# Macaron block: FFN passes over pairs of batches, another order of the opening, row maxima split before their transposition, two score banks and one PV bank

## The chip, the cores and the metric

One core of a Trainium2 chip runs the whole block. The metric is the device time in microseconds of one execution. Its engines each work through a queue of their own in order: TensorE (matmuls, with a sequencer that waits on semaphores), VectorE, ScalarE, GpSimd, and SyncE, which here only issues DMAs. They meet at semaphores alone.

## The reference

x is 8 batches of 512 tokens of 256 numbers, float32. Three steps follow each other, each behind a layer norm:

```python
x = x + 0.5 * ffn(layernorm(x))            # "first"
x = x + attn(layernorm(x))                 # rms norm, 16 heads of 16, causal softmax, Wo, + its own input
x = x + 0.5 * ffn(layernorm(x))            # "second", same weights
# ffn: 2 experts, FF = 1024; a token goes to the expert with the larger logit:
sel = argmax(softmax(x @ gate_w.T));  h = silu(x @ w_gate[sel].T) * (x @ w_up[sel].T)
out = (h @ w_down[sel].T) * probability of sel
```

## The kernel before, in words

**Order.** One function, `master()` (L113 and on), gives every piece of work a place on a scale of points and sorts by it; each engine then walks through the same sorted list and does its own part of each item. So the order is written by hand, and an engine that must wait holds all that is behind it on its queue. The loop is unrolled.

**FFN.** A pass takes one batch: its 512 tokens are sorted by expert, 640 places (5 slots of 128), expert 0 from the front and expert 1 from the back. A slot that may hold both experts' border takes its weights by a register (`flags`, `expert`). Each slot is two units (q = 0, 1) of half of FF; a unit is 48 gate and up matmuls of 128 columns (float32 as two float16 parts, three products), tanh on ScalarE (L628), two products on VectorE (L819, L823), a split into two parts on ScalarE (L634) and GpSimd (L579), and 12 down matmuls of 256 columns (L1028 to L1030). 16 passes (8 batches, first and second) of 10 units are 160 units, 6 points each. `PASSES` gives their order, `PASS_AT` their points.

**Route.** Ahead of a pass, `ROUTE_STEPS`: statistics on VectorE, their scale on GpSimd, normalisation on ScalarE (L608), dot products with the difference of the two gate rows on VectorE (L778), a prefix sum over tokens on TensorE (L981, L983, into ps_m), places (L797), four scatters on GpSimd (L538), one transposing load on SyncE (L444) into x_t. After the pass, four gathers on GpSimd (L553, `y_gather`) and the update of x on VectorE (L811, `x_update`).

**Attention.** Each batch is four parts (four heads each) of two pairs of heads; a pair is five fills of a PSUM bank. For each fill TensorE makes the scores (L1073, mask L1075) in ps_s, VectorE reduces them to row minima of the negated scores (L891, L895). At the part's end the minima are transposed on TensorE (L1081, `row_max`), split in three bf16 parts on VectorE (L904 to L908), saved to DRAM and loaded as three more rows of qt by three DMAs (L479, L482), so that the second, transposed scores (L1092, L1094, ps_st) come out with the maximum subtracted. ScalarE takes exp twice (L704, L705), VectorE or GpSimd the low part (L913, L584), TensorE multiplies with V (L1109, ps_v), VectorE normalises each pair (`o_norm`: L922, L924, L928). Part p starts at point 115 + 23 p. ps_s has one bank, ps_v two in turn; ps_m is shared by projections (L944), transposes, prefix sums and row maxima, each waiting until the one before is read.

**Opening.** The weights are loaded; VectorE finds the largest of the gate and up weights, then of the down weights, each gives a power of two as scale (`w_scale`, nine small instructions with a transpose L973 and a broadcast L975 on TensorE), and ScalarE and VectorE split 14 pieces into two parts (`w_split`, L599, L752). x_sorted is zeroed from x_t, which GpSimd sets to zero first; it also fills v_parts with ones.

## Time and profile before

| | us |
|---|---|
| median of 3 runs | 1386.37 (1385.54 to 1393.45) |
| profiled execution | 1373.07 |
| its span, first to last instruction | 1371.3 |
| TensorE, VectorE, ScalarE, GpSimd busy | 1139.5, 972.4, 710.8, 542.2 |
| mean granted TensorE clock | 0.938 of full |

The page shows one execution. Busy times are of instructions alone; a matmul's end is modelled, its time includes its way through the array, and the next one starts before it is over, so the distance from start to start tells the pace. The chain that ended last is cut short on this page at the last gather, so stages are read by windows.

### The profile page before, as it was taken

Reading aid. Unit: us, or ns where it says so; the run is one execution under the profiler, and the core shown is the slowest. Engines: PE = TensorE matmul, PEld = TensorE weight load, DVE = VectorE, ACT = ScalarE, POOL = GpSimd, SP = SyncE. Lnnn points to the kernel's source line nnn. Section 1 sums busy time; section 2 is a strip of 40 time slices with the busy share of each in tenths; the row PEclk is TensorE's granted clock in tenths of the full one; section 3 lists DMA queues with packets and bytes.
Section 4 is the critical chain, followed back from the end, with each engine's and each line's share of the span. In section 5 each row is a group of like instructions: output and inputs, shape, how many; then the busy total and the mean of one; then the engine's idle time right before and its main releaser. Section 6 shows DMA issues by size and latency. Waiting matters only on the chain. (4 is left out here: it accounts for less than half of the span.)

```text
span 1371.3 us, 40339 instructions
## 1 busy us (share of the span) xinstructions
PE 1139.5 (83%) x15028; PEld 983.4 (72%) x15028; DVE 972.4 (71%) x2064; ACT 710.8 (52%) x1311; POOL 542.2 (40%) x681
## 2 busy tenths in 40 slices
PE   0588889999888978899798888988999988989485
PEld 0467777777767866778587777876878877778374
DVE  7743548887786786888787878777888876766322
ACT  1523425656555654655465556645666654556221
POOL 6144344335425243344342434434445253344422
PEclk9999999999999999999899999999999999999788
DMA  9002222332123112322042223211312323120211
GB/s 324 6 25 63 84 80 65 79 100 74 49 64 92 39 39 78 106 71 65 28 119 60 68 73 89 78 35 54 108 41 72 98 62 70 33 58 32 44 39 43
DMA packets 118869, 96.21 MB, mean 70 GB/s; under 512 B 56096, under 2 KB 112672, under 8 KB 118688
## 3 DMA queue, kind: packets, MB, share of 16 engines
q1 hardware_dynamic: 101024, 66.36, 17.9%
q0 software_dynamic: 6144, 16.79, 4.2%
q10 hardware_dynamic: 11520, 10.49, 2.4%
q8 instruction: 134, 2.20, 0.7%
q14 instruction: 47, 0.39, 0.1%
HBM read 45.75 MB, written 37.36 MB: 61 GB/s over the span
## 5 line engine op out<-in xcount | busy, mean ns | idle before, releaser
L579 POOL TENSOR_TENSOR h_lo<-hid,h_hi 128x256 bf16<-128x256 f32 x320 | 223.1, 717 | 584.0 <-ACT h_hi L634 583.4
L704 ACT ACTIVATE area<-ps_st 128x512 f32<-128x512 f32 x320 | 189.8, 593 | 229.6 <-PE ps_st L1094 229.1
L1009 PE MATMUL ps_g<-x_t,w 128*128 128x128 f16 x1280 | 244.8, 226 | 31.2 <-DMA x_t<-x_sorted 14.5
L1011 PE MATMUL ps_u<-x_t,w 128*128 128x128 f16 x1280 | 245.7, 224 | 0.0
L1009 PE MATMUL ps_u<-x_t,w 128*128 128x128 f16 x1280 | 245.3, 224 | 0.2
L1011 PE MATMUL ps_g<-x_t,w 128*128 128x128 f16 x1280 | 245.1, 226 | 0.0
L1010 PE MATMUL ps_g<-x_t,w 128*128 128x128 f16 x1280 | 243.7, 225 | 0.0
L1010 PE MATMUL ps_u<-x_t,w 128*128 128x128 f16 x1280 | 243.4, 222 | 0.0
L895 DVE TENSOR_REDUCE row_min<-ps_s 128x1 f32<-128x512 f32 (+2 forms) x384 | 183.2, 504 | 60.7 <-PE ps_s L1075 60.1
L913 DVE TENSOR_TENSOR area<-area 128x512 f16<-128x512 f32 x256 | 186.8, 730 | 4.4 <-ACT area L705 2.1
L705 ACT ACTIVATE area<-ps_st 128x512 f16<-128x512 f32 x320 | 189.7, 593 | 0.0
L1028 PE MATMUL ps_y<-wd,h_hi 128*128 (+1 forms) x640 | 183.2, 286 | 6.9 <-POOL h_lo L579 6.4
L1029 PE MATMUL ps_y<-wd,h_hi 128*128 (+1 forms) x640 | 183.6, 287 | 0.0
L1030 PE MATMUL ps_y<-wd,h_lo 128*128 (+1 forms) x640 | 183.6, 287 | 0.0
L1009 PEld LDWEIGHTS ps_g<-x_t,w 128*128 (+1 forms) x1280 | 128.6, 101 | 51.5 <-issue 21.1
L1073 PE MATMUL ps_s<-kt,qt 96*128 96x512 bf16 (+3 forms) x512 | 138.9, 310 | 32.0 <-DVE row_min L895 31.0
L628 ACT ACTIVATE hid<-ps_g,g_scale 128x512 f32<-128x512 f32 x160 | 109.8, 686 | 103.8 <-PE ps_g L1011 100.4
L819 DVE SCALAR_TENSOR_TENSOR hid<-hid,ps_g 128x512 f32<-128x512 f32 x160 | 108.4, 677 | 68.8 <-ACT hid L628 68.8
L1092 PE MATMUL ps_st<-qt,kt 99*128 99x512 bf16 (+3 forms) x512 | 137.6, 307 | 10.6 <-ACT area L705 8.4
L1009 PEld LDWEIGHTS ps_u<-x_t,w 128*128 (+1 forms) x1280 | 126.6, 99 | 17.9 <-issue 2.4
L1011 PEld LDWEIGHTS ps_g<-x_t,w 128*128 (+1 forms) x1280 | 128.8, 101 | 2.3 <-issue 0.4
L1010 PEld LDWEIGHTS ps_g<-x_t,w 128*128 (+1 forms) x1280 | 129.1, 101 | 1.1
(146 smaller groups left out, 2636.5 us busy)
## 6 DMA issues: line engine op xcount, KB each, us to landing
qk_scratch<-area SPq DMA_DIRECT2D x32, 384.0 KB, 2.5
qt<-qk_scratch SPq DMA_DIRECT2D x192, 64.0 KB, 2.8
kt<-qk_scratch SPq DMA_DIRECT2D x192, 64.0 KB, 2.8
y_sorted<-ys ACTq DMA_DIRECT2D x80, 128.0 KB, 1.7
x_buf<-x SPq DMA_DIRECT2D x8, 512.0 KB, 4.9
out<-x_buf SPq DMA_DIRECT2D x8, 512.0 KB, 3.0
area<-w_down SPq DMA_DIRECT2D x4, 512.0 KB, 13.1
qt<-max_scratch SPq DMA_DIRECT2D x96, 4.0 KB
```

What stands on the lines that cost most here:

```text
L579: pool.tensor_tensor(h_lo[:, u % 2, c], hid[:, u % 2, c], h_hi[:, u % 2, c], ALU.subtract).then_inc(h_lo_done, 1)
L704: act.activation(p_f32[:, f % 3], ps_st[:], ACT.Exp, scale=-1.0)
L705: act.activation(p_hi[:, f % 4], ps_st[:], ACT.Exp, scale=-1.0).then_inc(exp_done, 1)
L895: ins = dve.tensor_reduce(row_min[:, p % 2, i, h + hh:h + hh + 1], ps_s[:, at:at + P * (i + 1)], AX.X, ALU.min)
L913: dve.tensor_tensor(p_lo[:, f % 4], p_f32[:, f % 3], p_hi[:, f % 4], ALU.subtract).then_inc(lo_done, 1)
L1009: pe.matmul(cols, w_hi, x_hi, start=kb == 0 and f == 0, stop=False, skip_group_check=True)
L1010: pe.matmul(cols, w_hi, x_lo, start=False, stop=False, skip_group_check=True)
L1011: ins = pe.matmul(cols, gate_up(u, kind, 1, kb, q * QF + f), x_hi, start=False, stop=kb == KB - 1, skip_group_check=True)
L1028: pe.matmul(ps_y[:, 0:D], hi, wd_lo, start=q == 0 and f == 0, stop=False, skip_group_check=True)
L1029: pe.matmul(ps_y[:, 0:D], hi, wd_hi, start=False, stop=False, skip_group_check=True)
L1030: ins = pe.matmul(ps_y[:, 0:D], lo, wd_hi, start=False, stop=q == 1 and f == QF - 1, skip_group_check=True)
L1073: pe.matmul(ps_s[:, at:at + keys], qt[0:ROWS, h, i * P:keys], kt[0:ROWS, h, 0:keys], start=n == 0, stop=False, skip_group_check=True)
```

## The change

Batches 2 and 3, 4 and 5 of the first FFN, first 7 with second 2, and second 3 with 4 are passed in pairs: 1024 tokens sorted together into 9 slots. 12 passes have 76 slots and 152 units. The route is done for each batch (an item), the second of a pair with the counts of the first added in the prefix sum; one transposing load follows. Route steps are spaced wider and start earlier, parts of attention stand 21 points apart instead of 23. In the opening, ScalarE sums the absolute down weights of each piece (`accum_out`) in place of VectorE's maximum, the second scale and most splits stand behind the first unit, zeroing takes a block of yt by 5, 9 and 4 DMAs, and only the ones column of v_parts is set. The row maxima are split by VectorE as 128 x 16 (`max_parts`), then all three parts are transposed by one bf16 matmul, copied by ScalarE, saved by one DMA and loaded by one. ps_s gets two banks in turn, ps_v keeps one. x gets a sixth buffer, routes a fourth.

```diff
-PASSES = [("first", 0), ("first", 1), ("first", 2), ("first", 3), ("first", 4), ("second", 0), ("second", 1),
-          ("first", 5), ("second", 2), ("first", 6), ("first", 7), ("second", 3), ("second", 4), ("second", 5),
-          ("second", 6), ("second", 7)]
-PASS_OF = {what: n for n, what in enumerate(PASSES)}
-XBUFS = 5
-ROUTES = 3
+
+PASSES = [[("first", 0)], [("first", 1)], [("first", 2), ("first", 3)], [("first", 4), ("first", 5)], [("second", 0)],
+          [("second", 1)], [("first", 6)], [("first", 7), ("second", 2)], [("second", 3), ("second", 4)],
+          [("second", 5)], [("second", 6)], [("second", 7)]]
+ITEMS = [(n, i, what, b) for n, batches in enumerate(PASSES) for i, (what, b) in enumerate(batches)]
+ITEM_OF = {(what, b): k for k, (n, i, what, b) in enumerate(ITEMS)}
+SLOTS = [T * len(batches) + 1 for batches in PASSES]
+
+ITEM_AT, SLOT_AT = [0], [0]
+for batches, slots in zip(PASSES, SLOTS):
+    ITEM_AT.append(ITEM_AT[-1] + len(batches))
+    SLOT_AT.append(SLOT_AT[-1] + slots)
+UNITS = [(n, s, q) for n, slots in enumerate(SLOTS) for s in range(slots) for q in range(2)]
+MAX_SLOTS = max(SLOTS)
+PLACES = MAX_SLOTS * P
+XBUFS = 6
+ROUTES = 4
...
-PASS_POINTS = UNIT_POINTS * UNITS
-PASS_AT = [PASS_POINTS * n for n in range(15)] + [916]
+SLOT_POINTS = 2 * UNIT_POINTS
+PASS_AT = [SLOT_POINTS * at for at in SLOT_AT[:4]] + [336, 396, 462, 522, 630, 738, 798, 865]
 PART_AT = 115
-PART_POINTS = 23
-FILL_POINTS = 2.3
-LEAD = 27
+PART_POINTS = 21
+FILL_POINTS = PART_POINTS / 10
+LEAD = 33
+PAIR_LAG = 9
...
+MAX_PARTS_AT = 21.5
...
-OUT_AT = [130.5, 132, 134, 136]
-ROUTE_STEPS = [("l_stats", 0, 0.0), ("l_stats", 1, 0.5), ("l_rstd", 0, 1.5), ("l_norm", 0, 3.0),
-               ("l_split", 0, 4.5), ("l_dlogit", 0, 4.6), ("l_exp", 0, 6.0), ("l_prefix", 0, 6.5),
-               ("l_pos", 0, 6.6), ("l_coef", 0, 7.8), ("l_scatter", 0, 9.0), ("l_load", 0, 13.0)]
+OUT_AT = [122, 123.5, 125.5, 127.5]
+ROUTE_STEPS = [("l_stats", 0, 0.0), ("l_stats", 1, 0.5), ("l_rstd", 0, 1.5), ("l_norm", 0, 4.0),
+               ("l_split", 0, 6.0), ("l_dlogit", 0, 6.5), ("l_exp", 0, 10.5), ("l_prefix", 0, 11.0),
+               ("l_pos", 0, 11.2), ("l_coef", 0, 13.0), ("l_scatter", 0, 14.5), ("l_load", 0, 19.0)]
...
-            ("l_pos", 0): -55.8, ("l_coef", 0): -43.2, ("l_scatter", 0): -55, ("l_load", 0): -54}
-SPLIT_AT = [-50, -49, -48, -47, -46, -45.5, -45, -44.5, -43, -42, -2, 0, 14, 16]
+            ("l_pos", 0): -55.8, ("l_coef", 0): 20, ("l_scatter", 0): -55, ("l_load", 0): -54}
+MAX_AT = [-59, -58, -57, -56, -55, -54, -53, -52, -51.2, -51, -46.8, -46.6]
+SCALE_AT = [-50.5, 3.9]
+SPLIT_AT = [-50, -49, -48, -47, -46, 1.2, 2.2, 4, 5, 7, 13, 15, 26, 28]
...
+    for k, (n, i, what, b) in enumerate(ITEMS):
+        end = PASS_AT[n] + SLOT_POINTS * SLOTS[n] + 5.2 * i
+        put(end + 8, "y_gather", k)
+        put(end + 13, "x_update", k)
+        at = PASS_AT[n] - LEAD - PAIR_LAG * (len(PASSES[n]) - 1 - i)
...
+        put(part_at(p, MAX_PARTS_AT), "max_parts", p)
         put(part_at(p, ROW_MAX_AT), "row_max", p)
...
-        ps_s, ps_st, ps_m = bank("ps_s"), bank("ps_st"), bank("ps_m")
-        ps_v = [bank(f"ps_v{n}") for n in range(2)]
-        ps_o = [v[:, 0:2 * T * VW].rearrange("p (h i c) -> p h i c", h=2, i=T) for v in ps_v]
+        ps_st, ps_v, ps_m = bank("ps_st"), bank("ps_v"), bank("ps_m")
+        ps_s = [bank(f"ps_s{n}") for n in range(2)]
+        ps_o = ps_v[:, 0:2 * T * VW].rearrange("p (h i c) -> p h i c", h=2, i=T)
...
-                    zero(0)
+                    sp.wait_ge(zero_ready, 1)
+                    zero(0, range(SLOTS[0]))
...
+                    sp.wait_ge(scattered, 64 * ITEM_AT[n + 1])
+                    if n >= 2:
+                        sp.wait_ge(u_done, 2 * SLOT_AT[n - 1])
+                    sp.dma_start_transpose(x_t_of(n), x_sorted[n % 2][0:P * SLOTS[n], :]).then_inc(xt_loaded, 16)
                     if n == 0:
-                        zero(1)
-                    sp.wait_ge(scattered, 64 * (n + 1))
-                    if n >= 2:
-                        sp.wait_ge(u_done, UNITS * (n - 1))
-                    sp.dma_start_transpose(x_t[n % 2][:], x_sorted[n % 2]).then_inc(xt_loaded, 16)
...
-                    sp.wait_ge(max_parts_done, p + 1)
-                    sp.dma_start(max_scratch[g].rearrange("r i h s -> (i h) r s"), max_parts[:]).then_inc(max_saved, 16)
+                    sp.wait_ge(max_rows_done, p + 1)
+                    sp.dma_start(max_scratch[g], max_rows[:]).then_inc(max_saved, 16)
                     sp.wait_ge(max_saved, 16 * (p + 1))
-                    for n in range(3):
-                        sp.dma_start(qt[ROWS + n:ROWS + n + 1, heads].rearrange("o h (i s) -> o h i s", i=T),
-                                     max_scratch[g, n:n + 1].rearrange("o i h s -> o h i s")
-                                     ).then_inc(max_in, 16)
+                    sp.dma_start(qt[ROWS:ROWS + 3, heads].rearrange("r h t -> r (h t)"),
+                                 max_scratch[g].rearrange("(r n) s -> r (n s)", r=3)).then_inc(max_in, 16)
...
-            pool.memset(x_t[0][:], 0.0).then_inc(zero_ready[0], 1)
+            pool.memset(yt[:, 0, :], 0.0).then_inc(zero_ready, 1)
...
-                        pool.memset(x_t[1][:], 0.0).then_inc(zero_ready[1], 1)
-                        link(pool.memset(v_parts[0][:], 1.0))
-                        pool.memset(v_parts[1][:], 1.0).then_inc(v_ones_ready, 1)
-                        pool.wait_ge(v_ones_ready, 1)
...
+                if what == "w_max" and st[1] >= GU_PIECES:
+
+                    w = st[1]
+                    act.wait_ge(w_in[w], 16)
+                    if w > GU_PIECES:
+                        act.wait_ge(w_sum_done, w - GU_PIECES)
+                    act.activation(flat(hid[:]), stage[w], ACT.Abs,
+                                   accum_out=w_max[:, w:w + 1]).then_inc(w_sum_done, 1)
...
+                elif what == "row_max":
+                    p = st[1]
+                    act.wait_ge(mt_done, p + 1)
+                    if p:
+                        act.wait_ge(max_saved, 16 * p)
+                    act.activation(max_rows[:], ps_m[0:3 * HG * T, 0:P], ACT.Copy).then_inc(max_rows_done, 1)
...
+                    ins = dve.tensor_tensor(place[r][:], high_place[:], ps_m[:, 0:T], ALU.add)
+                    if i == len(PASSES[p]) - 1:
+                        between = slice(0, SLOTS[p] - 2)
+                        ins = dve.scalar_tensor_tensor(out=of_slot[p % 3][:, between], in0=edges[:, between],
+                                                       scalar=ps_m[0:1, T:T + 1], in1=strides[:, between],
+                                                       op0=ALU.is_ge, op1=ALU.mult)
+                    ins.then_inc(l_pos, 1)
...
-                    if f == 0 and p >= 2:
-                        dve.wait_ge(mt_done, p - 1)
                     h = 2 * (f // KINDS)
                     if f % KINDS == KINDS - 1:
-                        ins = dve.tensor_reduce(row_min[:, p % 2, 1, h:h + 2], ps_s[:].rearrange("p (h n) -> p h n", h=2),
+                        ins = dve.tensor_reduce(row_min[:, p % 2, h:h + 2, 1], ps_s[f % 2][:].rearrange("p (h n) -> p h n", h=2),
                                                 AX.X, ALU.min)
                     else:
                         for hh, i, at in S_FILLS[f % KINDS]:
-                            ins = dve.tensor_reduce(row_min[:, p % 2, i, h + hh:h + hh + 1], ps_s[:, at:at + P * (i + 1)],
+                            ins = dve.tensor_reduce(row_min[:, p % 2, h + hh, i:i + 1], ps_s[f % 2][:, at:at + P * (i + 1)],
...
-                elif what == "row_max":
+                elif what == "max_parts":
                     p = st[1]
-                    dve.wait_ge(mt_done, p + 1)
+                    dve.wait_ge(max_done, FILLS * (p + 1))
                     if p:
-                        dve.wait_ge(max_saved, 16 * p)
-                    maxima = ps_m[0:T * HG, 0:P]
-                    link(dve.tensor_scalar(max_parts[:, 0, :], maxima, -1.0, None, ALU.mult))
-                    link(dve.scalar_tensor_tensor(out=max_rest[:], in0=maxima, scalar=-1.0, in1=max_parts[:, 0, :],
+                        dve.wait_ge(mt_done, p)
+                    minima = row_min[:, p % 2].rearrange("p h i -> p (h i)")
+                    link(dve.tensor_scalar(max_parts[:, 0, :], minima, -1.0, None, ALU.mult))
+                    link(dve.scalar_tensor_tensor(out=max_rest[:], in0=minima, scalar=-1.0, in1=max_parts[:, 0, :],
...
-                    if FILLS * p + f:
-                        pe.wait_ge(max_done, FILLS * p + f)
+                    if FILLS * p + f >= 2:
+                        pe.wait_ge(max_done, FILLS * p + f - 1)
...
-                    pe.wait_ge(max_done, FILLS * (p + 1))
-                    pe.transpose(ps_m[0:T * HG, 0:P], row_min[:, p % 2].rearrange("p i h -> p (i h)"), ident[:]).then_inc(mt_done, 1)
+                    pe.wait_ge(max_parts_done, p + 1)
+                    pe.matmul(ps_m[0:3 * HG * T, 0:P], max_parts[:].rearrange("p r n -> p (r n)"), ident16[:],
+                              start=True, stop=True).then_inc(mt_done, 1)
...
-                    if f % KINDS == 0 and n >= 2 * KINDS:
-                        pe.wait_ge(o_summed, n // KINDS - 1)
+                    if f % KINDS == 0 and n:
+                        pe.wait_ge(o_summed, n // KINDS)
```

## Rows read from the trace of the kernel before

**Rows 1.** Head of the page: busy time and share of the span by engine.

```profile
PE 1139.5 (83%) x15028; PEld 983.4 (72%) x15028; DVE 972.4 (71%) x2064; ACT 710.8 (52%) x1311; POOL 542.2 (40%) x681
```

**Rows 2.** Windows by stage: busy us (x instructions) of each engine, granted clock, DMA.

```profile
core 0: us, PE busy (x) PEld busy (x) DVE busy (x) ACT busy (x) POOL busy (x), PEclk, DMA share, GB/s
47.50:176.70 129.20, 106.66 (x1219) 92.92 (x1220) 59.53 (x124) 50.17 (x83) 46.81 (x67) 0.91 0.17 50
176.70:1268.60 1091.90, 967.23 (x13039) 833.76 (x13036) 844.66 (x1817) 625.46 (x1174) 442.20 (x540) 0.95 0.25 68
1000.00:1100.00 100.00, 92.17 (x1239) 79.67 (x1236) 85.14 (x185) 61.62 (x116) 40.12 (x51) 0.98 0.25 72
```

**Rows 3.** Waits of TensorE, 176.7 to 1268.6: us in total, times, longest.

```profile
PE ps_s L1073 <- DVE row_min L895: 31.0, 32, 4.6
PE ps_m L981 <- DVE neg_abs L788: 22.8, 6, 6.6
...
PE ps_m L944 <- DVE max_parts L908: 8.5, 6, 2.1
...
PE ps_m L981 <- DVE area L865: 8.2, 2, 5.4
```

**Rows 4.** The same, 47.5 to 176.7.

```profile
PE ps_m L981 <- DVE neg_abs L788: 10.8, 2, 5.5
```

**Rows 5.** Window of a stretch after a wait, columns as in rows 2.

```profile
403.00:409.80 6.80, 5.59 (x33) 4.14 (x33) 6.29 (x16) 1.91 (x4) 0.00 (x0) 0.50 0.42 122
```

**Rows 6.** Timeline, first gate matmuls of two units in succession: start, duration us.

```profile
1346.29 0.22 PE L1009 MATMUL ps_g<-x_t,w 128*128 128x128 f16 x1
...
1350.28 0.22 PE L1009 MATMUL ps_g<-x_t,w 128*128 128x128 f16 x1
```

**Rows 7.** Costliest groups by form, whole span: busy us, mean ns, idle before.

```profile
L823 DVE SCALAR_TENSOR_TENSOR hid<-hid,ps_u 128x512 f32<-128x512 f32 x160 | 109.9, 687 | 20.8 <-PE ps_u L1011 15.1 <-DVE hid L819 0.4
...
L819 DVE SCALAR_TENSOR_TENSOR hid<-hid,ps_g 128x512 f32<-128x512 f32 x160 | 108.4, 677 | 68.8 <-ACT hid L628 68.8
...
L640 ACT ACTIVATE ys<-ps_y 128x256 f32<-128x256 f32 x80 | 30.8, 385 | 76.2 <-PE ps_y L1030 76.0
...
L788 DVE SCALAR_TENSOR_TENSOR neg_abs<-dlogit 128x4 f32<-128x4 f32 x16 | 3.4, 213 | 0.0
```

**Rows 8.** Window of the mixed stage, VectorE's instructions on max_parts alone.

```profile
176.70:1268.60 1091.90, 41.18 (x128) 0.95 0.25 68
```

**Rows 9.** Timeline of the opening: start, duration in us.

```profile
25.72 3.50 DVE L733 TENSOR_SCALAR w_two<-w_exp 1x2 int32<-1x2 int32 x1
...
26.47 2.74 POOL L543 MEMSET v_parts<- 128x3136 bf16 x1
...
29.01 4.09 SPq L444 DMA_TRANSPOSE x_t<-x_sorted  x1
...
47.57 0.29 PE L1009 MATMUL ps_g<-x_t,w 128*128 128x128 f16 x1
...
54.70 0.10 PEld L1009 LDWEIGHTS ps_g<-x_t,w 128*128 128x128 f16 x1 [2.61 <-DVE hid L819]
```

**Rows 10.** DMA issues: count, median us to landing.

```profile
x_t<-x_sorted SPq DMA_TRANSPOSE x16, 6.4
```

**Rows 11.** Timeline of two handovers of PV: reciprocal and next PV.

```profile
845.20 0.36 PE L1109 MATMUL ps_v<-v_parts,area 128*128 128x49 bf16 x8
...
849.26 0.20 DVE L924 RECIPROCAL recip<-ps_v 128x8 f32<-128x8 f32 x1
...
1247.05 0.20 DVE L924 RECIPROCAL recip<-ps_v 128x8 f32<-128x8 f32 x1
...
1248.20 0.36 PE L1109 MATMUL ps_v<-v_parts,area 128*128 128x49 bf16 x8
```

**Rows 12.** TensorE's wait behind the last PV, and the last pass's first matmul.

```profile
PE ps_m L981 <- DVE neg_abs L788: 8.7, 1, 8.7
...
1305.91 0.29 PE L1009 MATMUL ps_g<-x_t,w 128*128 128x128 f16 x1 [13.05 <-DMA x_t<-x_sorted]
```

More of the change, by code:

```diff
@@ L217, in macaron @@
         xs = sb("xs", [P, T, 2, D], F16)
-        x_t = [sb(f"x_t{n}", [P, 2 * KB, PLACES], F16) for n in range(2)]
+        x_t = [sb(f"x_t{n}", [P, 2 * KB * PLACES], F16) for n in range(2)]
         ys = [sb(f"ys{n}", [P, D], F32) for n in range(2)]
@@ L715, in _ @@
                 what = st[0]
-                if what == "w_max":
+                if what == "w_max" and st[1] < GU_PIECES:
                     w = st[1]
@@ L998, in _ @@
                             pe.wait_ge(w_ready, GU_PIECES)
-                        if u % UNITS == 0 and what == "gate":
+                        if s == 0 and q == 0 and what == "gate":
                             pe.wait_ge(xt_loaded, 16 * (n + 1))
-                            pe.wait_ge(l_pos, n + 1)
+                            pe.wait_ge(l_pos, ITEM_AT[n + 1])
                         if u:
```

216 lines of the change are left out of this document (115 added, 101 removed).

## The prediction

> **What bounds the kernel now.** I read the head of the page, then the windows by stage, then TensorE's waits, then the costs on VectorE. The head [rows 1] says TensorE 83% busy, VectorE 71%: neither is full, so the bound must be looked for by stage. The windows [rows 2] cut the span at the first gate matmul (47.5 us), at the first score (176.7) and behind the last PV (1268.6). The stage from 176.7, attention interleaved with FFN, holds 1091.9 of 1371.3 us, with TensorE busy 967 and VectorE 845 us (77%). Its pace is not fixed: TensorE at 89% on the mean, in the stretch 1000:1100 both engines are higher, 92% and 85%. So the stage is limited by two in-order engines that wait for each other in turn, with slack to win when waits go.
>
> TensorE's waits in that stage [rows 3] are, of the 125 us that it stands idle there: 31.0 for the row-minimum reduction (S has one bank), 31.0 for the prefix matmul L981 (22.8 and 8.2), 8.5 for ps_m held by the row maxima; the rest is small. After such a stop the granted clock falls: the longest stop at the prefix in this stage that the projection's VectorE part ends, 5.4 us, is followed by 403.0 to 409.8 at 0.50, the lower level (1.2 GHz) [rows 3, 5]. The stage's mean is 0.95 [rows 2].
>
> **The change part by part.** The passes had 16 x 5 slots; now four pairs have 9 slots and eight single batches 5: 76 slots, 152 units for 160. One unit's TensorE work at the full clock is 48 gate and up and 12 down matmuls, from the first gate matmul at 1346.29 to the next unit's at 1350.28 [rows 6]: 4.0 us. On VectorE it is 677 + 687 ns [rows 7].
>
> Opening. Before, the first gate matmul (47.57) stands behind the second weight scale, because the order puts all of it first; the first scale itself is late by a VectorE instruction on two numbers that takes 3.50 us beside a memset on GpSimd and ends with it at 29.2 [rows 9]; the next one runs beside the next memset. These memsets go, the scan of the down weights goes to ScalarE, and the second scale and most splits go behind the first gate. Then what comes last is x_t: issued at 29.01, median 6.4 to landing [rows 9, 10], so 35.4. The splits are no later: the scale's chain started that instruction at 25.72 and is then some 1 us from its end, and the first splits need about 4 us behind it. Unit 0's gate and up matmuls hold two thirds of a unit's columns, 2.7 of the 4.0 us, and twice that at the lower clock, 5.4; its VectorE work ends near 41.5, the second scale, nine small instructions of some 0.21 us [rows 7], near 43.4, and unit 1 starts there against 54.70 [rows 9]: 11 us earlier. Several splits now stand between units on VectorE, which works 59.5 of 129 us in this stage [rows 2]; I take off 1. **Minus 10.** Its ends: minus 4 (if the work only moved behind unit 0 and is paid there; the memsets' part stays won) and minus 12 (35.4 against 47.6). Zeroing is now by 5, 9 and 4 DMAs from one small block, behind the load of pass 0: nothing waits for it until the scatter of pass 1; cover, the 60 us of pass 0.
>
> Route. Steps before the prefix matmul are spread over 11 points for 6.5, at a lead of 33 for 27. A point of the mixed stage is 1091.9/775 = 1.41 us (points 115 to 890), so the chain has 6 us more, and the longest wait is 6.6 [rows 3]. In the stage from 47.5 to 176.7 two waits cost 10.8 [rows 4]; I take three quarters, **minus 8**, as the extra item of the first pair is prepared there. In the mixed stage 31.0: I take two thirds, 20, plus 8 for the clock behind them. The bounds: nothing (the wait moves to the next user), and 31 + 3.4 x 8 = 58 when all go with their dips.
>
> For the clock the row says 0.95 over 1091.9 us, so 10% of the time was at the lower level. The Trainium skill's TensorE page (TensorE: Matmul & The Clock Gate, Terms) prices throttled time at its length times the share of pulses taken away. By that the stage would give back 55 us if no stop were left, not my 8; I hold to 8, as only a third of the stops are touched.
>
> Pairs. The mixed stage runs from point 115 to about 823 (parts every 21 points) instead of 890; with 6 points per unit it holds 118 units for 129. Eleven fewer at 4.0 us and 10% for clock and gaps: **minus 48**. The parts' own work stays. Ends: minus 0 (attention's chain has a pace of its own) and minus 15.0/0.77 = 19 if only VectorE's 11 x 1.364 counts, up to 67 x 1.41 = 94 (the pace per point kept, though each point holds more attention). I stay near the unit's TensorE time, as TensorE is the busier of the two. A transposing load of nine slots for five: 6.4 x 1.8 = 11.5 us [rows 10], issued 14 points = 20 us ahead: hidden. The sync queue is held by its issue for 4.09 x 1.8 = 7.4 us at most [rows 9]; the maxima behind it have 8 points = 11 us before the transposed scores: at no cost, and 2 us per hit if that cover goes (four pairs). Prefix matmuls of a second item: four more small ones, under 0.1 us each. The gather of a pair waits for nine slots, its deadline is 30 points away. A sixth x buffer only loosens.
>
> Row maxima. The four VectorE instructions of 16 x 128 take 41.2 us in 32 parts, 1.29 each part [rows 8]; they become four of 128 x 16, and the nearest row is one of 128 x 4 at 213 ns [rows 7]: 0.85 us at that price, at most the old 1.29. I take 0.7, since some of the like are shorter (the chain of nine above): 19 us less, off VectorE. A copy on ScalarE, at most 385 ns, the price of 128 x 256 [rows 7], x 32 = 12 us on an engine with 466 us idle in the stage [rows 2]. ps_m is held by the copy alone, so the 8.5 us of L944 go in part: **minus 3**. One load replaces three. The new copy waits for TensorE at the head of ScalarE's queue; behind it stand exp and tanh, which wait for TensorE anyway.
>
> Two S banks. A score fill waits for the reduction two fills back, 2.1 points = 3 us more slack, against waits of 31.0 in 32 pieces, longest 4.6 [rows 3]. Most go as waits at this place, but VectorE has the same work and is late at the next: I take 12; ends 0 and 31. The Trainium skill (same page, HAM oscillation — how this bites in real kernels) tells of a kernel where PSUM double buffering on top brought no further gain. By that the gain would be 12 us smaller; it is a rival below. The rows have a wait on this very bank, so I keep 12.
>
> One PV bank. The first PV of a pair must now wait for the reciprocal of the pair before. Before, it did not. Two handovers [rows 11]: in one the reciprocal ends at 1247.25 and the next pair's PV starts at 1248.20, 0.95 us of slack; in the other it ends at 849.46 and that PV started at 845.20, 4.3 us too early. So the price per handover lies between 0 and 4.3, 63 times. What stands behind the waiting PV is all of TensorE's queue: gates, scores, transposed scores, and so ScalarE's exp. I take 0.8 gross, nearer the calm one, 50 us, of which half is time in which TensorE would have waited for VectorE elsewhere: **plus 25**.
>
> Mixed stage: -48 - 20 - 8 - 3 - 12 + 25 = -66, 1026 us. VectorE's work there falls to 845 - 15 - 19 = 811, a share of 79%, between the two shown.
>
> Tail. From the last PV (1268.6) the chain of out-projection, statistics, prefix, load and gate (1305.91) lasts 37.3 us, with TensorE idle 8.7 and 13.05 us [rows 12]. Now pass 10 still has 5.8 units instead of 2: four more, 16 us, fit in those 21.7. The last pass and its way out stay. **Minus 3** for a shorter stop ahead of the last gate (0 to 6).
>
> Sum: -10 - 8 - 66 - 3 = -87. The profiled execution lasts 1373.07 us (span 1371.3), 13 under the runs' median of 1386.37; the same step from the median gives **1299**.
>
> **The rivals.**
> VectorE sets the pace: the mixed stage keeps its VectorE share of 77.4%: 811/0.774 = 1048, minus 44. Total -65: 1321. For it: VectorE is late in the handover at 849 [rows 11]; against: 85% in 1000:1100. Chance 0.20.
> The second S bank gives nothing, as VectorE is as late at the next place: -75, 1311. For it: the same reductions stay on a VectorE that is 77% busy; against: the waits on this bank are many and short [rows 3]. Chance 0.10. The page's sentence on PSUM buffers in the Trainium skill is of this kind.
> The waits really go, and the clock stays up: 85.1% everywhere, 953 us, -139, total -160: 1226. Against it: PV's bank. Chance 0.07. The skill's price of throttled time fits in this case alone.
> The change's fewer units buy nothing: attention's chain keeps 34.1 us per part and units only filled holes. Then -21 of opening, start and tail stay: 1365. For it: TensorE has 125 us idle in the stage; against: it is busy 89%. Chance 0.08.
> Slower: the single PV bank. Without it the sum is -112. Slower by 1% begins at 126/63 = 2.0 us net per handover; at 2.5 it is +158 - 112 = +46: 1432. It decides where VectorE's order has a route's or a projection's work ahead of the normalisation; the bank then stops TensorE, ScalarE's exp behind it comes late, and VectorE is late again. For it: the handover at 849; against: the other has slack. Chance 0.08.
>
> **How the numbers follow.** Forecast 0.47 with its own range 1270 to 1328 (opening 8, pairs 20, PV 25 either way, not all together). The range 1258 to 1352 leaves out the slower case, the 1365 one in part and most of the 1226 one. A difference under 1% can't be told from none here. Faster by more: 0.47 + 0.10 + 0.20 + 0.07 and a quarter of 0.08, 0.86 (the 1365 is 1.5% below, but its range reaches across 1%); within 1%: 0.06; slower: 0.08, the last rival's.
>
> **What would show it.** First gate near 35 to 38 and the first score near 157 to 160; 152 units on VectorE, 118 of them in the mixed stage; that stage near 1026; L981's waits under 15 us in all and the L1073 group's under 20; a new wait of the first PV on the reciprocal of 20 to 60 us; the maxima at under 0.25 us each. A mixed stage over 1060, or PV waits over 100 us, would prove the sum wrong.

## The result, and the profile after

The changed kernel's median is 1367.8 us (1365.91 to 1371.26, 4 runs) against 1387.49 of the kernel before (4 runs): a ratio of 0.9854 [0.9817, 0.989], 1.5% faster. 1299 was forecast, with a range from 1258 to 1352. The gain is a quarter of the forecast, and the time lies outside the range.

The windows by stage of the changed kernel, cut at its first gate matmul, first score and last PV (columns as in rows 2):

```profile
0.00:34.40 34.40, 0.86 (x8) 0.43 (x9) 22.32 (x46) 14.41 (x20) 12.26 (x39) 1.00 0.90 313
34.40:176.40 142.00, 113.04 (x1230) 96.77 (x1230) 71.56 (x158) 56.32 (x92) 56.65 (x76) 0.90 0.21 64
176.40:1261.70 1085.30, 926.36 (x12349) 795.75 (x12346) 821.09 (x1767) 613.72 (x1171) 418.56 (x508) 0.94 0.24 66
1261.70:1369.40 107.70, 82.19 (x987) 71.14 (x983) 35.58 (x70) 27.97 (x49) 36.42 (x49) 0.91 0.15 43
```

Against [rows 2]: the first gate comes 13 us earlier, the first score 0.3 us; the mixed stage is 6.6 us shorter, the tail 5.0 us longer. That is 1.9 us in all where the medians say 19.7, because the first trace of before was 13 us under its own runs and this one is 3.5 us over. So I profiled both again, on chips where before's median is 1370.5 and 1368.5; those two traces lie 3.9 and 5.2 us under the medians of their kernels, and the stages are compared in them. Before, second trace (mixed stage, tail):

```profile
176.80:1262.50 1085.70, 961.53 (x13039) 829.24 (x13037) 845.50 (x1817) 625.87 (x1174) 441.96 (x540) 0.96 0.25 68
1262.50:1364.80 102.30, 64.37 (x771) 56.18 (x767) 30.34 (x62) 22.20 (x39) 32.62 (x43) 0.82 0.17 42
```

Changed, second trace:

```profile
173.40:1232.90 1059.50, 907.73 (x12350) 782.86 (x12348) 824.76 (x1767) 613.93 (x1171) 419.08 (x508) 0.95 0.25 68
1232.90:1339.70 106.80, 82.82 (x986) 71.38 (x983) 35.80 (x70) 27.95 (x49) 36.42 (x49) 0.91 0.15 44
```

Of the 25.1 us between the spans (1364.8 and 1339.7), 3.4 lie ahead of the first score, 26.2 in the mixed stage, and the tail loses 4.5. In the mixed stage TensorE's busy time falls by 53.8 us, but its **idle time** (length less busy) rises from 124.2 to 151.8. That pair of numbers is what the rest of this document follows; in the first pair of traces it is 124.7 and 158.9. Busy time is no exact measure either: the same 12,350 matmuls of the mixed stage count as 904.6 to 926.4 us in nine traces with pairs, the 13,039 without pairs as 959.2 to 972.0 in six. So the fall in busy time is 41 us by the first pair of traces and 54 by the second, and a difference in idle time of less than some 15 us says little by itself. The units went as planned, and the waits did not.

TensorE's waits in the mixed stage of the changed kernel, first trace (columns as in rows 3):

```profile
PE ps_v L1163 <- DVE recip L972: 59.6, 31, 5.9
PE ps_st L1146 <- ACT area L748: 20.8, 15, 5.4
...
PE ps_v L1163 <- POOL area L612: 10.0, 5, 3.5
PE ps_m L1134 <- DVE area L915: 7.6, 7, 2.3
PE ps_m L992 <- DVE xt_lo L898: 6.1, 7, 1.5
...
PE ps_m L1031 <- DVE area L915: 3.2, 1, 3.2
...
PE ps_s L1126 <- DVE row_min L939: 2.5, 2, 1.8
```

Against [rows 3] the three waits that the change was to take away are nearly gone: S from 31.0 to 3.8 us (with a row of 1.3 for L943), the prefix (L1031 now) from 31.0 to 3.6, the row maxima (8.5) replaced by L1134's. In their place stands one wait of 59.6 us (61.5 in the second trace), of the first PV of a pair on the reciprocal. A handover is the way of the PV bank from its last reader, the reciprocal of one pair, to the first PV of the next. Counted over the 63 handovers, 39 first PVs start within 0.25 us of the reciprocal's end, so they had waited; before, 47 started ahead of it. The longest, on TensorE:

```profile
944.99 0.49 PE L1163 MATMUL ps_v<-v_parts,area 128*128 128x49 bf16 x8 [5.87 <-DVE recip L972]
```

and VectorE in the same stretch:

```profile
941.10 1.41 DVE L822 CUSTOM_DVE_ANT_0 junk<-xn_f,w_diff 128x256 bf16<-128x256 f32 x1
...
944.10 0.15 DVE L833 SCALAR_TENSOR_TENSOR neg_abs<-dlogit 128x4 f32<-128x4 f32 x1
944.18 0.55 DVE L970 TENSOR_REDUCE o_sum<-ps_v 128x128 f32<-128x384 f32 x1
944.64 0.20 DVE L972 RECIPROCAL recip<-ps_v 128x8 f32<-128x8 f32 x1
```

The route's dot products (3 us) stand ahead of the normalisation on VectorE, and TensorE stands for them. Then the clock falls; the windows behind it:

```profile
945.00:948.00 3.00, 3.00 (x28) 2.43 (x29) 1.43 (x4) 1.60 (x3) 0.17 (x1) 0.54 0.03 5
948.00:952.00 4.00, 4.00 (x79) 3.71 (x77) 2.47 (x5) 1.75 (x4) 2.29 (x3) 1.00 0.00 0
```

The opening of the changed kernel, VectorE (start, duration):

```profile
25.22 0.16 DVE L777 TENSOR_SCALAR w_two<-w_exp 1x2 int32<-1x2 int32 x1
...
42.01 0.69 DVE L873 SCALAR_TENSOR_TENSOR hid<-hid,ps_u 128x512 f32<-128x512 f32 x1
42.62 0.15 DVE L770 TENSOR_REDUCE w_max<-w_max 128x1 f32<-128x4 f32 x1
...
45.31 1.28 DVE L796 SCALAR_TENSOR_TENSOR w<-kt,w_scale,w 128x1024 f16<-128x1024 f32 x1
```

and TensorE:

```profile
34.39 0.27 PE L1062 MATMUL ps_g<-x_t,w 128*128 128x128 f16 x1 [8.58 <-issue]
...
46.80 0.28 PE L1062 MATMUL ps_g<-x_t,w 128*128 128x128 f16 x1 [1.97 <-issue]
```

The instruction on two numbers that took 3.50 us beside the memset [rows 9] takes 0.16 without it. Unit 0 starts at 34.4, unit 1 at 46.8 against 54.70.

### The profile page after: what moved, and what is told of

The parts are those of the page before. It is cut to its first block and busy times, and to the rows that moved or that the text cites. A ratio compares the mean times of both kernels' runs of the same rounds, so it can differ in the third digit from the quotient of the medians.

```text
span 1369.4 us, 39636 instructions
## 1 busy us (share of the span) xinstructions
PE 1122.4 (82%) x14564; PEld 964.1 (70%) x14564; DVE 950.5 (69%) x2040; ACT 712.4 (52%) x1331; POOL 523.9 (38%) x671
## 5 line engine op out<-in xcount | busy, mean ns | idle before, releaser
L607 POOL TENSOR_TENSOR h_lo<-hid,h_hi 128x256 bf16<-128x256 f32 x304 | 219.1, 741 | 582.1 <-ACT h_hi L671 580.6
L1062 PE MATMUL ps_g<-x_t,w 128*128 128x128 f16 x1216 | 240.4, 230 | 35.9 <-issue 27.3
L943 DVE TENSOR_REDUCE row_min<-ps_s 128x1 f32<-128x512 f32 (+2 forms) x384 | 183.3, 505 | 87.5 <-PE ps_s L1128 84.3
L1064 PE MATMUL ps_g<-x_t,w 128*128 128x128 f16 x1216 | 240.0, 230 | 3.1 <-issue 3.1
L1064 PE MATMUL ps_u<-x_t,w 128*128 128x128 f16 x1216 | 238.8, 226 | 2.9 <-issue 2.9
L1063 PE MATMUL ps_g<-x_t,w 128*128 128x128 f16 x1216 | 239.0, 229 | 1.9 <-issue 1.9
L1062 PE MATMUL ps_u<-x_t,w 128*128 128x128 f16 x1216 | 238.8, 227 | 2.1 <-issue 1.7
L1063 PE MATMUL ps_u<-x_t,w 128*128 128x128 f16 x1216 | 237.0, 225 | 1.2 <-issue 1.2
L961 DVE TENSOR_TENSOR area<-area 128x512 f16<-128x512 f32 x256 | 192.1, 750 | 11.7 <-ACT area L748 11.6
L1163 PE MATMUL ps_v<-v_parts,area 128*128 128x49 bf16 x2560 | 120.8, 187 | 76.1 <-DVE recip L972 59.6
L1081 PE MATMUL ps_y<-wd,h_hi 128*128 (+1 forms) x608 | 171.3, 282 | 6.2 <-POOL h_lo L607 3.9
L1163 PEld LDWEIGHTS ps_v<-v_parts,area 128*128 128x128 f16 x2560 | 102.8, 98 | 101.7 <-issue 50.8
L1083 PE MATMUL ps_y<-wd,h_lo 128*128 (+1 forms) x608 | 171.6, 282 | 0.0
L1082 PE MATMUL ps_y<-wd,h_hi 128*128 (+1 forms) x608 | 171.4, 282 | 0.0
L1062 PEld LDWEIGHTS ps_g<-x_t,w 128*128 (+1 forms) x1216 | 125.1, 103 | 55.9 <-issue 42.9
L1146 PE MATMUL ps_st<-qt,kt 99*128 99x512 bf16 (+3 forms) x512 | 140.3, 312 | 21.3 <-ACT area L748 20.8
L665 ACT ACTIVATE hid<-ps_g,g_scale 128x512 f32<-128x512 f32 x152 | 104.6, 688 | 92.8 <-PE ps_g L1064 72.7
L869 DVE SCALAR_TENSOR_TENSOR hid<-hid,ps_g 128x512 f32<-128x512 f32 x152 | 103.1, 678 | 62.3 <-ACT hid L665 62.3
```

Source lines behind the costliest of these rows:

```text
L607: pool.tensor_tensor(h_lo[:, u % 2, c], hid[:, u % 2, c], h_hi[:, u % 2, c], ALU.subtract).then_inc(h_lo_done, 1)
L943: ins = dve.tensor_reduce(row_min[:, p % 2, h + hh, i:i + 1], ps_s[f % 2][:, at:at + P * (i + 1)], AX.X, ALU.min)
L961: dve.tensor_tensor(p_lo[:, f % 4], p_f32[:, f % 3], p_hi[:, f % 4], ALU.subtract).then_inc(lo_done, 1)
L1062: pe.matmul(cols, w_hi, x_hi, start=kb == 0 and f == 0, stop=False, skip_group_check=True)
L1063: pe.matmul(cols, w_hi, x_lo, start=False, stop=False, skip_group_check=True)
L1064: ins = pe.matmul(cols, gate_up(u, kind, 1, kb, q * QF + f), x_hi, start=False, stop=kb == KB - 1, skip_group_check=True)
```

## The experiments

Two theories stood against each other after the result. **H**: the single PV bank, handed over late by VectorE, eats the gain. **V**: VectorE's pace is the bound, and each bank only shows where it is late. Ratios are to the kernel before, run beside them on the same chip; before's own median was 1389.7, 1370.5, 1368.5 and 1386.6 us on the four chips, so times of different chips are compared by ratio alone; figures in square brackets are 95% intervals. "Mixed" is the stage between first score and last PV, "idle" its length less TensorE's busy time.

**Banks as before, rest changed** (run twice).

```diff
-        ps_st, ps_v, ps_m = bank("ps_st"), bank("ps_v"), bank("ps_m")
-        ps_s = [bank(f"ps_s{n}") for n in range(2)]
+        ps_s, ps_st, ps_m = bank("ps_s"), bank("ps_st"), bank("ps_m")
+        ps_v = [bank(f"ps_v{n}") for n in range(2)]
...
-                    if FILLS * p + f >= 2:
-                        pe.wait_ge(max_done, FILLS * p + f - 1)
+                    if FILLS * p + f:
+                        pe.wait_ge(max_done, FILLS * p + f)
...
-                    if f % KINDS == 0 and n:
-                        pe.wait_ge(o_summed, n // KINDS)
+                    if f % KINDS == 0 and n >= 2 * KINDS:
+                        pe.wait_ge(o_summed, n // KINDS - 1)
```

> The changed kernel with the banks as before: S one, PV two in turn; all else as changed. Theory H (the handover of the one PV bank eats the gain): in the changed kernel TensorE waited 59.6 us for the reciprocal ahead of PV, before it did not, and the old waits on the S bank (31 us) come back; so 20 to 35 us faster than the changed kernel, 1333 to 1348, with the mixed stage near 1050. Rival P (the mixed stage has a pace of its own, about 34 us per part, and waits only move): within 8 us of the changed kernel, 1360 to 1376, with other waits of the same sum.

> The changed kernel with the banks as before, again, beside its base. Theory H: 10 to 20 us under the changed kernel, as between the first two calls (ratios 0.975 and 0.985). Rival: the two ratios came from different calls, and side by side they are within 5 us.

Measured: 1352.68, ratio 0.975 [0.9721, 0.978]; again, beside the changed kernel (0.9845 [0.9823, 0.9867]), 1340.46, 0.9809 [0.9764, 0.9854]. So the swap of banks costs 0.4 to 1.0% here, the lower figure (6.2 us, on one chip) with overlapping intervals. Its waits in the mixed stage (second run):

```profile
PE ps_s L1126 <- DVE row_min L943: 52.2, 40, 5.7
...
PE ps_s L1126 <- DVE row_min L939: 12.9, 6, 5.7
```

That is 65 us of waits on the one S bank (55.9 in the first run), where the changed kernel has 61.5 on the one PV bank. I read both as ways to wait for the same VectorE. Idle is 145.4 us here and 151.7 in the first run, against 151.8. Before, with the sparser order, that S bank cost 31.0 [rows 3].

**The swap alone, on the kernel before**, and **without pairs**: the old 16 passes, distances, lead and route steps, with new opening and row maxima, once with the new banks and once with the old.

```diff
-PASSES = [[("first", 0)], [("first", 1)], [("first", 2), ("first", 3)], ...
+PASSES = [[item] for item in [("first", 0), ("first", 1), ("first", 2), ...
-PART_POINTS = 21
+PART_POINTS = 23
-LEAD = 33
+LEAD = 27
```

> The kernel before with only the banks swapped: S two in turn, PV one. Theory H: handovers cost 60 to 80 us of TensorE stops against 31 saved, so 15 to 40 us slower than before, 1402 to 1427. Rival P: within 8 us of before, 1379 to 1395.

> The changed kernel without pairs: 16 passes of 5 slots, 160 units, with the points, the part distance of 23, the lead and the route steps of before; the opening, the row maxima and the banks are as changed. Theory H: the opening and the maxima give 10 to 15, the banks take 15 to 40: 1385 to 1415. Rival P: 1370 to 1387, as the opening alone shows.

> As the run without pairs, and with the banks as before too: before with the new opening and row maxima alone. Theory H: 1365 to 1378 (opening 13 us at the first gate, maxima 19 us less on VectorE). Rival P, with the opening's gain taken back ahead of the first score as in the changed kernel: 1380 to 1390.

Measured: the swap on the kernel before 1423.09, 1.0232 [1.0187, 1.0277]; without pairs 1394.01, 1.0024 [0.9996, 1.0052] with the new banks and 1376.34, 0.9911 [0.988, 0.9942] with the old. So the swap costs 2.3% on the kernel before, 1.1% without pairs and 0.4 to 1.0% in the changed kernel: it is a gain nowhere, and the same edit has three prices. On the kernel before the first PVs wait 61.3 us for the reciprocal and the 31.0 on S are gone, 30 more in all, and the time is 33 us longer. Opening and row maxima are worth 0.9%, 13 us. Mixed stage without pairs, new banks:

```profile
171.60:1281.90 1110.30, 959.19 (x13039) 825.79 (x13037) 840.05 (x1817) 630.77 (x1206) 443.48 (x540) 0.96 0.24 67
```

old banks:

```profile
173.40:1271.80 1098.40, 972.04 (x13040) 831.49 (x13038) 838.17 (x1817) 630.30 (x1206) 442.67 (x540) 0.96 0.24 67
```

Idle 151.1 and 126.4: near the value of before with the old banks, near the changed kernel's with the new. The one S bank waits 21.3 us in the second of them; its main row:

```profile
PE ps_s L1126 <- DVE row_min L943: 20.6, 27, 3.0
```

**Both kernels profiled again** (before, changed).

> The kernel before once more, for a second trace. Its first profiled execution was 13 to 16 us under the median of its timed runs, the other kernels' were within 10. If that execution was an exception, the second trace has a span near 1385 and a mixed stage near 1105 us; if it is how the traced execution always stands, near 1371 and 1092.

> The changed kernel itself once more. Two calls had medians of 1389.7 and 1370.5 us for the same kernel before, so only runs of one call are compared; this is the base for the three beside it. Both theories: 0.982 to 0.989 of before.

Measured: 1366.59 in one run, 3.9 us under the median of before on that chip, so the 13 us of the first trace were the exception; and 1346.70, 0.9845 [0.9823, 0.9867], close to the result's own ratio.

**Less work on VectorE by moving it** (banks as before; GpSimd makes two of five low parts instead of one), **less by leaving it out**, and **less work on TensorE**.

```diff
-                elif what == "p_lo" and st[2] % KINDS < KINDS - 1:
+                elif what == "p_lo" and st[2] % KINDS < KINDS - 2:
```

```diff
-                    dve.tensor_tensor(p_lo[:, f % 4], p_f32[:, f % 3], p_hi[:, f % 4],
+                    dve.tensor_tensor(p_lo[:, f % 4, 0:P], p_f32[:, f % 3, 0:P], p_hi[:, f % 4, 0:P],
```

```diff
-                        ins = pe.matmul(cols, gate_up(u, kind, 1, kb, q * QF + f), x_hi, start=False,
-                                        stop=kb == KB - 1, skip_group_check=True)
```

> The changed kernel with the banks as before, and with the low part of exp for two of five fills on GpSimd instead of one: 64 x 0.73 = 47 us less on VectorE, 64 x 1.19 = 76 more on GpSimd (38% busy). Theory V (the mixed stage follows VectorE's work: what it is late with, TensorE waits for at the next bank): 15 to 35 us faster than with the banks as before, 1318 to 1338. Rival H' (the stage follows the waiting hand-overs and latencies, not the amount of work): within 8 us of 1353, or slower, as the low part then comes 0.46 us later to PV.

> The changed kernel with VectorE making only the first 128 of the 512 columns of the low part of exp in its fills, the rest is zero: the output is less exact. VectorE has about 256 x 0.45 = 115 us less work. Theory V: 50 to 90 us faster. If TensorE's work sets the pace: under 20 us.

> The changed kernel without one of the three products (low weights by high x) of gate and up: its output is less exact. TensorE has 152 x 16 x 0.0557 = 135 us less to stream, nothing else changes. If TensorE's work sets the pace, 100 us or more faster: below 1268. Theory V: its work is half hidden, 40 to 75 us faster. If it is only the other engines, under 20.

Measured: 1348.91, 0.9881 [0.9815, 0.9947]; 1308.96, 0.9574 [0.951, 0.9637]; 1292.09, 0.9451 [0.9372, 0.9529]. Moving bought nothing over the banks as before (0.975 and 0.9809). It is a weak test of V, though: VectorE's busy time in the mixed stage is 801.3 us against 824.2 and 828.4 with the banks as before, 23 to 27 less for the 47 expected, because other instructions take longer (L822 726 ns for 625, a low part on VectorE 794 for 772). GpSimd needs 1.21 us for the low part:

```profile
L612 POOL TENSOR_TENSOR area<-area 128x512 f16<-128x512 f32 x128 | 154.3, 1210 | 74.4 <-ACT area L748 74.1
```

Mixed stage of the kernel with less VectorE work:

```profile
174.30:1200.80 1026.50, 904.60 (x12349) 781.83 (x12347) 719.77 (x1767) 613.41 (x1171) 397.35 (x508) 0.95 0.26 70
```

and with less TensorE work:

```profile
168.50:1202.50 1034.00, 832.50 (x10478) 701.33 (x10476) 829.27 (x1767) 611.22 (x1172) 418.66 (x508) 0.91 0.25 69
```

VectorE does 105 us less there than in the changed kernel and the ratio falls from 0.9845 by 0.027, 37 us of 1370 (28 to 46 by the intervals; V had 50 to 90): 0.35 us per us taken. TensorE loses 2,432 matmuls of 128 columns, 134 us at the 55 ns from start to start, and the ratio falls by 0.039, 54 us (43 to 65; V had 40 to 75): 0.4. Neither engine is the bound of the whole; each us is worth a third or a little more. By stages it isn't even: against the second trace of the changed kernel 1,872 of the matmuls, 103 us, leave the mixed stage and it is 25.5 us shorter (some 36, if one allows for the two traces lying 5.7 us over and 5.2 under their medians), while 249, 13.7 us, leave the tail and it is 13.3 us shorter.

**Old route steps in the changed kernel.**

```diff
-ROUTE_STEPS = [..., ("l_dlogit", 0, 6.5), ("l_exp", 0, 10.5), ("l_prefix", 0, 11.0), ..., ("l_load", 0, 19.0)]
+ROUTE_STEPS = [..., ("l_dlogit", 0, 4.6), ("l_exp", 0, 6.0), ("l_prefix", 0, 6.5), ..., ("l_load", 0, 13.0)]
```

> The changed kernel with the route's steps spaced as before (prefix 6.5 points behind the statistics instead of 11, load at 13 instead of 19), at the new lead. If the wider spacing is worth what its 31 us of vanished prefix waits say: 20 to 30 us slower than the changed kernel. Theory V (waits on VectorE's late work only move to the next bank): the prefix waits come back, others fall, and the time is within 8 us.

Measured: 1352.89, 0.9877 [0.9849, 0.9905] against 0.9845 on the same chip: 6 us slower by the medians, with intervals that overlap. Its windows from first gate to last PV:

```profile
34.10:184.70 150.60, 113.12 (x1229) 96.95 (x1230) 72.87 (x158) 56.77 (x92) 57.03 (x76) 0.83 0.24 67
184.70:1241.70 1057.00, 911.55 (x12350) 785.73 (x12347) 823.06 (x1767) 615.12 (x1171) 418.77 (x508) 0.94 0.24 67
```

and a wait in the mixed stage:

```profile
PE ps_m L1031 <- DVE neg_abs L833: 21.0, 8, 6.5
```

This is the cleanest result on the route. The prefix waits are back with 21 us, and the mixed stage is 1057.0 us long against 1059.5 without them. Three other waits, in the changed kernel's second trace and then with the old steps:

```profile
PE ps_v L1163 <- DVE recip L972: 61.5, 33, 5.9
...
PE ps_st L1146 <- ACT area L748: 13.8, 5, 5.4
PE ps_v L1163 <- POOL area L612: 12.5, 7, 3.5
```

```profile
PE ps_v L1163 <- DVE recip L972: 52.0, 30, 6.3
...
PE ps_v L1163 <- POOL area L612: 7.5, 7, 2.2
PE ps_st L1146 <- ACT area L748: 6.7, 5, 2.2
```

These three fall by 21.6 us and L1134's rises by 4.0: most of what the prefix waits take is given back by others. The lead of 33 points stayed, so this run tells of the spacing of the steps alone. What the new steps save is in the start stage, where the first score comes 11.3 us earlier (173.4 for 184.7).

**The handover spaced**: the first PV of a pair 1.3 points later, the normalisation 0.7 points earlier, so that 3.1 points lie between them for 1.1; run twice, then each half alone, then both without pairs (there 3.3 points for 1.3).

```diff
-            put(at + PV_LAG * FILL_POINTS - 0.2, "pv", p, f)
+            put(at + PV_LAG * FILL_POINTS - 0.2 + 1.3 * (f % KINDS == 0), "pv", p, f)
...
-                put(at + PV_LAG * FILL_POINTS + 0.8, "o_norm", p, f // KINDS)
+                put(at + PV_LAG * FILL_POINTS + 0.1, "o_norm", p, f // KINDS)
```

> The changed kernel with the first PV of each pair 1.3 points later and the normalisation 0.7 points earlier in VectorE's order, so 2.0 points = 2.7 us more for the one PV bank to be read. Theory H: most of the 76 us of stops at that place go, and 8 to 20 us of the time, what the second PV bank gives. Theory V taken alone: the stops move to the S banks and the other users, within 5 us.

> The spaced hand-over (first PV 1.3 points later, normalisation 0.7 points earlier) once more, as the base for the three beside it. 0.960 to 0.970 of before, as in the call before.

> The changed kernel with only the first PV of each pair 1.3 points later. If the gain is that TensorE has other work in the time of the hand-over: most of it is here, 0.965 to 0.975 of before.

> The changed kernel with only the normalisation 0.7 points earlier in VectorE's order. If the gain is that VectorE reads the bank ahead of its other late work: most of it is here, 0.965 to 0.975; if the other half does it: 0.980 to 0.986, as the changed kernel.

> No pairs (16 passes, part distance, lead and route steps of before), with the new opening, maxima and banks and with the spaced hand-over. Without pairs the single PV bank cost 1.1% and more; if the spaced hand-over takes that away and pairs with their route are worth 1.7 to 1.8% at either state of the banks: 0.978 to 0.986 of before. If the pairs' worth was only hidden by the hand-over and is nearer the forecast 5%: 1.00 or above.

Measured: 1322.39, 0.9644 [0.9609, 0.9679] beside the changed kernel's 0.9845; again 1330.50, 0.9609 [0.9548, 0.9669]; later PV alone 1347.56, 0.9731 [0.9645, 0.9817]; earlier normalisation alone 1342.37, 0.97 [0.9631, 0.9768]; without pairs 1363.42, 0.9843 [0.9754, 0.9931]. **This version beats both kernels**, the kernel before by 3.6 to 3.9%, the changed one by 1.8% (24.3 us, on one chip). Each half alone has its waits for the reciprocal at about half, 30.7 and 25.8 us, and a ratio between the two, which the intervals don't set clearly apart from either. The mixed stage of both halves together, and its wait:

```profile
174.70:1217.90 1043.20, 918.76 (x12349) 792.09 (x12347) 830.25 (x1767) 615.50 (x1171) 424.40 (x508) 0.94 0.25 69
```

```profile
PE ps_v L1163 <- DVE recip L972: 8.7, 11, 1.3
```

13 of 63 first PVs start right behind the reciprocal instead of 40, the wait falls from 61.5 to 8.7 us, idle from 151.8 to 124.4, near the value of before. The stage is 16.3 us shorter in these two traces, where the medians differ by 24.3: this trace lies 4.2 us over its median, the changed kernel's 5.2 under. The second run, from first gate to the end:

```profile
34.50:178.80 144.30, 112.92 (x1229) 96.20 (x1230) 71.38 (x158) 56.49 (x92) 56.56 (x76) 0.89 0.22 64
178.80:1221.40 1042.60, 912.49 (x12349) 783.97 (x12347) 825.33 (x1767) 615.14 (x1171) 425.18 (x508) 0.96 0.25 69
1221.40:1328.30 106.90, 82.11 (x987) 70.66 (x983) 35.58 (x70) 27.91 (x49) 36.49 (x49) 0.94 0.15 43
```

and the same without pairs, on the same chip:

```profile
34.10:171.00 136.90, 107.97 (x1221) 91.05 (x1222) 65.74 (x136) 53.60 (x86) 47.73 (x66) 0.90 0.17 50
171.00:1259.90 1088.90, 962.66 (x13038) 830.46 (x13036) 832.99 (x1817) 631.35 (x1206) 443.39 (x540) 0.95 0.25 68
1259.90:1361.40 101.50, 64.01 (x770) 56.01 (x766) 30.33 (x62) 22.19 (x39) 32.58 (x43) 0.83 0.15 43
```

Here pairs, part distance and route together take 46.3 us from the mixed stage, give 7.8 us back ahead of the first score and 5.4 in the tail: 33 us of span, as the medians say (1363.42 less 1330.50). Idle is 126.2 without them, with 28.3 us of prefix waits, and 130.1 with them, with 8.0: here too the prefix waits that went left no less idle time.

## Why the prediction was wrong, point by point

The forecast for the mixed stage was minus 66, of which minus 48 was work and minus 18 the balance of waits (minus 20, 8, 3 and 12, plus 25). The second pair of traces has minus 54 of work and plus 28 of waits. The terms below that failed are the route and its clock (28 us), the opening with the start stage (15) and the tail; what the new, closer order costs in waits was missing.

**"Pairs ... minus 48": right with the handover spaced, too much without.** Busy time fell by 41 to 54 us, and pairs with their distances and route steps took 46.3 from the mixed stage in the pair of runs just shown. Without the spaced handover the same edit takes 25.0 in the traces (1110.3 to 1085.3, two chips of like medians); these lie 8.3 us under and 3.5 over their medians, so some 37 is nearer. With the banks of before it takes 32.6 (1098.4 to 1065.8, one chip), some 29 when allowed for in the same way. So a fifth of the 46 needs the spaced handover, and with the old banks over a third is missing.

**"One PV bank ... plus 25": right in size**, and the gross wait of 61.5 is 0.98 us per handover for the 0.8 taken. Spacing the handover gives back 27.4 us of idle, and 24.3 us of the median, though spacing isn't the same edit as a second PV bank. My two terms for the swap of banks together, plus 13, can be put to the swap itself: it cost 5 to 14 us in the changed kernel, 16 to 18 without pairs and 33 on the kernel before. The slower rival's place was seen as well, route work ahead of the normalisation (5.87 us at 944.99), but at about 1 us on the mean, not 2.5.

**"Route ... I take two thirds, 20, plus 8 for the clock": this step failed.** The waits went as forecast (3.6 us left), and nothing came of it: with 21.0 us of them put back the stage is 2.5 us shorter, not longer, and three other waits are 21.6 us smaller. The bound "nothing (the wait moves to the next user)" stood in the prediction and is what the runs bear out. The granted clock went from 0.96 to 0.95, not up. By the Trainium skill (TensorE: Matmul & The Clock Gate, Terms), throttled time costs its length times the share of pulses taken away. In the start stage the old route steps put the clock at 0.83 for 150.6 us against 0.91 for 139.0, which by that rule is an estimate of 25.6 against 12.5 us lost, 13 us. The stage is 11.6 us longer, which fits, but TensorE's busy time there differs by only 1.7 us (111.46 and 113.12): it is the stops that made it longer, and the low clock stands beside them. So my 8 should not have been in the sum; the rule's 55 us for a stage without any stop is tested by no run here.

**"Two S banks ... I take 12": not shown either way.** The waits at this place went (31.0 to 3.8), but none of the idle time did: with the PV wait spaced away it is 124.4 us against 124.2 before, and that is after route, row maxima and S bank together, forecast at 43. This is against the sum and not against this term, since no run changes the S bank alone. What the sum lacked is a term for the new order's own waits: with the banks of before in both, the one S bank waits 21.3 us without pairs and 55.9 to 65.1 with them, and idle rises from 126.4 to 145.4 and 151.7. That it is the closer fills (2.1 points for 2.3) that do this is my reading, as pairs and route steps change with them. Against one S bank in the same closer order two may well be worth the 12: two S banks with the spaced PV bank are 18.1 us faster than one S bank with two PV banks (1322.39 and 1340.46, one chip). The Trainium skill (same page, HAM oscillation — how this bites in real kernels) reports no further gain of PSUM double buffering in its kernel. For the S bank no run here shows whether that holds. A bank taken away from PV, with S given one, cost 1.1 to 2.3% without pairs, so the sentence doesn't carry over to a buffer that is removed.

**"Row maxima: minus 3", VectorE 19 us less: mis-sized.** Four instructions of 128 x 16 take 36.17 us in 32 parts, where 41.18 stood before [rows 8]: 283 ns each where I took 175, so VectorE saves 5 us and not 19. The window, instructions on max_parts alone (TensorE's, its weight loads, VectorE's):

```profile
176.40:1261.70 1085.30, 7.60 (x32) 3.18 (x32) 36.17 (x128) 0.94 0.24 66
```

The price of one was right: 100 of the 128 take 173 ns on the mean. The other 28 take 675, and every one of them runs beside a GpSimd instruction, mostly a low part (L607, L612). One such pair, GpSimd's and VectorE's:

```profile
225.41 1.16 POOL L612 TENSOR_TENSOR area<-area 128x512 f16<-128x512 f32 x1
...
225.52 1.08 DVE L955 CAST max_parts<-max_rest 128x16 bf16<-128x16 f32 x1
```

The second trace has 26 of 128, 774 ns on the mean. The wait behind the row maxima (8.5 us) went, and L1134 waits 7.6 us in its stead. What the maxima gave in time isn't separated from the opening: both together gave 13 us.

**"Opening ... minus 10" and "minus 8" in the start stage: failed.** The first gate came where it was forecast (34.4 for 35.4), but unit 1 only 7.9 us earlier, not 11: the second scale starts on VectorE at 42.62, behind unit 0's products, where I had it done by 43.4, and a split of 1.28 us from 45.31 stands between it and unit 1. Without pairs the first score comes at 171.0 to 173.4, 3 to 6 us earlier than before, near the lower end that I named; with pairs at 173.4 to 178.8, where the second item's route is prepared in the same stage. That this route takes the rest is my reading, and no run isolates it. The wait at the prefix [rows 4] is nearly gone (1.0 us), and two others stand in the same stage:

```profile
PE ps_m L992 <- DVE area L915: 5.9, 1, 5.9
...
PE ps_m L992 <- DVE place L843: 3.2, 1, 3.2
```

Forecast minus 18, measured minus 3.4.

**"Tail ... minus 3": wrong in sign.** It is 4.5 us longer. TensorE's idle time there fell from 37.9 to 24.0 us, but 18.5 us of busy time came in, the units that now stand behind the last PV: they fill the hole [rows 12] and run over it.

The sum: 62 us lie between forecast and traces, 46 of them in the waits of the mixed stage, 15 ahead of it, 7.5 in the tail, less 6 that units gave beyond the forecast. The 46 are the route's 28, the 15 of S bank and row maxima together, and 3 more. The 6 is within the error of busy time, and the 15 within reach of it. Of the rivals, the one with 1365 came nearest in time and is refuted in its cause: fewer units, with their distances, took 25 to 46 us from the mixed stage; its nearness is luck. V, VectorE as the one bound, is refuted by its 0.35 us per us. H holds for the 24 to 27 us that the unspaced handover costs, but those were in the forecast; the miss lies beside it, in waits that were counted as gains and in the closer order's own.

**Open** stays why the same swap of banks costs between 0.4% and 2.3%: the order's density and the row maxima differ between these kernels, and I haven't separated them. Nor did I run the old route steps, or one S bank, with the handover spaced. TensorE's idle time of 124 to 130 us comes back in four kernels and six traces (before, without pairs with the old banks, and the three runs with the spaced handover), within the error of busy time; what sets that value is not shown.

## What to carry to other kernels

When two in-order engines are busy 75 to 90% each, don't count a named wait as a gain before a run has shown it: here 21 us of prefix waits were worth nothing, and of 53 us of waits at the handover 24 came back. Work that left all engines together was worth up to its full time on the busiest (11 units, 44 us of TensorE: 46 with the handover spaced, some 29 to 37 without); work that left one engine alone a little over a third. When a buffer goes from two to one, look at once at the distance in the order between its last reader and its next writer and widen it from both sides: here that was worth 24 us, more than the whole change (20 to 22). Ask also what a closer order does to the buffers that stay single. Compare stages in traces that lie as near to the median of their own runs as each other.

## What was not expected of the hardware

The same kernel has medians of 1386 to 1390 us on some chips and 1368 to 1371 on others, some 1.4% apart, with the ratio of changed to before the same on both (0.9854 and 0.9845). With 134 us of TensorE's work left out, the granted clock of the mixed stage falls from 0.95 to 0.91, and the kernel is faster all the same. An instruction on 1x2 numbers takes 0.16 us where it took 3.50 beside a memset of another tile on GpSimd, and of the 128 small ones on max_parts those beside a GpSimd low part can take 1.08 us for 0.17.
